# Cross-attention and feed-forward kernel: scores on four 32-row tiles, and PSUM dealt out anew

## The chip, the cores and the metric

The kernel runs on one core of one Trainium2 chip. A core has five engines that run side by side, each through its own queue in order: TensorE (PE, matrix products, which only it can write to PSUM), VectorE (DVE), ScalarE (ACT), GpSimd (POOL) and SyncE (SP, which here only issues DMAs). They are ordered among each other by semaphores alone. The metric is the device time of one execution, in microseconds.

## The reference, cut to what matters

16 batches (B) of 128 positions and 128 features; 8 heads of 16 features. The first part is an mLSTM cell with q = layernorm(x) and k = v = ctx, the second a feed-forward net with weights +1 and -1.

```python
log_f = jax.nn.log_sigmoid(fg)                  # gates from q, k, v
cs = jnp.cumsum(log_f, axis=1)
log_D = where(tril, cs[:, :, None] - cs[:, None, :], -inf) + ig[:, None, :]
max_log_D = jnp.max(log_D, axis=-1, keepdims=True)
D_mat = jnp.exp(log_D - max_log_D)
qk = jnp.einsum('hsd,htd->hst', qh, kh) / np.sqrt(DH)
C = qk * D_mat
normalizer = jnp.maximum(jnp.abs(C.sum(-1, keepdims=True)), jnp.exp(-max_log_D))
h = jnp.einsum('hst,htd->hsd', C / (normalizer + EPS), vh)
x = x + (h - mean(h)) / sqrt(var(h) + 1e-5) * ln_scale
x = x + ffn(layernorm(x))     # [x, -x] -> 512 -> relu -> 512 -> relu -> 128
```

## The kernel before

Everything is written out by hand: each engine has its own program, and each instruction that needs another engine's result waits on a semaphore by count. The 16 batches go through a software pipeline of 23 slots (`for n in range(SLOTS)`). In slot n, PE makes the scores of batch n and the weighted values of batch n-1 and turns them back (transposes them); ACT makes the exponentials of batch n+1; DVE multiplies scores and exponentials of batch n (make_c) and then normalizes batch n-1 and adds batch n-2 to the residual.

**Groups.** The gates are made for four batches at a time (group g). turn(g, 1) and turn(g, 0) transpose ctx and the normalized x of the four batches on PE into PSUM, turn_out on ACT copies them to qcT. gates(g) on PE makes the gate rows, forget_min(g) on DVE takes min(f, 0), gate_logs(g) on ACT the abs, exp and ln of log-sigmoid, gate_scans(g) on DVE the two running sums and maxima, turn_a and turn_m transpose the two results, take_a, take_m and em_guard on ACT copy them out. The DMA queue of SP spreads the eight heads of q into q_heads and the running maxima to all partitions (maxb). For the first four batches (DIRECT) the maxima are not loaded by DMA: bar and spread_max lay the distances into PSUM on PE, and ACT's decay reads them there. Group 2 is turned in slot 3, its gates stand in slot 4, its scans in slot 4, its turn_a and turn_m in slot 5; group 3 the same in slots 7, 8 and 9.

**Scores.** scores(n), L386 to L398: two products, each over a 64-row tile of q_heads (four heads laid out in blocks), 512 columns wide, fp32, into the two banks of pS. Each fp32 product is two passes in the profile (64 records for 32 products).

**PSUM.** Eight banks: pG (transposes and gates), pS (two), pO (weighted values and what is turned back), pX (x2's transposes and one bank of the direct distances), pF (three, for the feed-forward sums, which take them in turn, L242). The direct distances of two batches at a time lie in pF and pX.

**Feed-forward part.** Pair f (two batches) has five sums ffn(f, m): m = 0, 1 the first layer, 2, 3 the second, 4 (LAST) the third; ffn_of_slot says in which slot each stands: (f-1, 3), (f, 0), (f, 1) in the slot that opens a pair, then (f-1, LAST), (f, 2). ACT's high(f, m) writes the relu as fp16, DVE's low(f, m) the rest. Before it DVE's norm_x makes x2, ACT's x2_take_high and POOL's x2_take_low split it, turn_x2(n) on PE transposes one batch a slot, and take_x2T(f) on DVE (L824) copies a pair to SBUF.

The order on each engine in a slot is that of its loop: PE L506 to L535, ACT L648 to L676, DVE in the loop behind gate_scans(0), POOL at the end.

## Time and profile before

| | us |
|---|---|
| Three runs | 126.08, 124.39, 125.08 (median 125.08) |
| The profiled execution: its time | 124.36 |
| Its span, first to last instruction | 122.6 |
| PE busy | 106.3 |
| DVE busy | 98.6 |
| ACT busy | 77.1 |
| POOL busy | 62.9 |
| Mean granted clock of TensorE | 0.968 |

The span is 1.8 us shorter than the execution's own time, which has a start and an end around it. Busy times count records of the engine that do not overlap; they say nothing about which engine another waits for. "Idle before" in a row is the time the engine stood still before that instruction, with the one that released it. The granted clock is a share of 2.4 GHz; 0.5 is 1.2 GHz.

### The profile page before, as it was taken

The page shows a single profiled execution, that of the slowest core. Times are in us where ns is not written, and L with a number is a line of the kernel's source. Part 1 is how long each engine was busy: PE and PEld are TensorE (multiplying, and loading weights), DVE is VectorE, ACT ScalarE, POOL GpSimd, SP SyncE. Part 2 cuts the span into 40 slices and gives each one's busy share as a digit, 9 for nine tenths or more (in the row PEclk, how much of TensorE's full clock was granted, in tenths as well). Part 3 has the DMA queues.
Part 4 walks back from the last instruction along what each step waited for, and adds up shares of the span by engine and source line. Part 5 has one row for each costly group of instructions (what it writes and reads, how often), then busy time and mean ns, then how long its engine had stood idle before and what let it go on. Part 6 is the DMA issues. An engine that isn't in the chain of part 4 may idle for free.

```text
span 122.6 us, 3374 instructions
## 1 busy us (share of the span) xinstructions
PE 106.3 (87%) x1127; PEld 75.1 (61%) x1127; DVE 98.6 (80%) x334; ACT 77.1 (63%) x227; POOL 62.9 (51%) x145
## 2 busy tenths in 40 slices
PE   4898999998486379999979999999999999898960
PEld 4897676473242143658665685765866767696950
DVE  5445977969699999783999799999899999847341
ACT  4013589468899673959597996986987352525110
POOL 6944770345738788282736484684661464520000
PEclk9999999999999955899999999999999999999998
DMA  2885375269213179001215970100100100110101
GB/s 68 229 225 113 53 215 120 48 227 372 88 25 58 47 318 322 32 0 22 50 22 154 331 268 1 43 8 0 43 5 0 43 0 8 43 43 0 51 0 43
DMA packets 13105, 11.45 MB, mean 93 GB/s; under 512 B 2064, under 2 KB 11552, under 8 KB 13088
## 3 DMA queue, kind: packets, MB, share of 16 engines
q1 hardware_dynamic: 11792, 10.82, 29.4%
q10 hardware_dynamic: 1296, 0.42, 1.5%
q8 instruction: 9, 0.15, 0.4%
q14 instruction: 8, 0.07, 0.2%
HBM read 8.94 MB, written 1.25 MB: 83 GB/s over the span
## 4 chain that ended last, share of the span: by engine, by line
POOL 42%; issue 28%; PE 19%; DVE 7%; ACT 1%; POOLq 1%; DVEq 0%
POOL maxb L975 10%; POOL rs_x L946 7%; POOL rs_h L946 6%; PE pF L468 6%; POOL x2p L994 5%; PE pF L376 4%; POOL rs_q L956 3%; PE pS L396 3%; POOL ve_x L945 3%; POOL ve_h L945 2%; PE pF L447 2%; POOL vals L967 2%; POOL q_heads L1022 1%; DVE xn L714 1%; DVE h L842 1%
## 5 line engine op out<-in xcount | busy, mean ns | idle before, releaser
L468 PE MATMUL pF<-h,w 128*128 128x256 f16 x256 | 30.3, 273 | 0.0
L599 ACT ACTIVATE dmat<-maxb,aT 128x128 f32<-128x128 f32 x96 | 29.3, 390 | 0.0
L468 PEld LDWEIGHTS pF<-h,w 128*128 128x128 f16 x256 | 24.7, 98 | 2.6
L842 DVE SCALAR_TENSOR_TENSOR h<-pF,h 128x512 f16<-128x512 f32 x32 | 20.9, 680 | 5.8 <-ACT h L622 5.8
L622 ACT ACTIVATE h<-pF 128x512 f16<-128x512 f32 x32 | 18.1, 591 | 9.8 <-PE pF L468 9.8
L748 DVE SCALAR_TENSOR_TENSOR cmat<-pS,dmat 128x512 f32<-128x512 f32 x32 | 20.5, 682 | 1.9 <-PE pS L396 1.9
L994 POOL TENSOR_TENSOR x2p<-x,x2p 128x128 f16<-128x128 f32 x16 | 6.9, 428 | 26.5 <-ACT x2p L614 26.5
L396 PE MATMUL pS<-q_heads,qcT 64*128 64x512 f32 x64 | 19.0, 672 | 0.0
L410 PEld LDWEIGHTS pO<-cmat,vals 128*32 128x32 f32 x256 | 6.3, 112 | 11.8 <-issue 9.9
L975 POOL TENSOR_SCALAR_AFFINE_SELECT maxb<-maxb 128x1024 f32<-128x1024 f32 x12 | 13.2, 1099 | 0.4 <-DMA maxb<-running_max 0.4
L410 PE MATMUL pO<-cmat,vals 128*32 128x128 f32 x256 | 10.7, 287 | 1.7 <-POOL vals L967 1.7
L608 ACT COPY oT<-pO 128x256 f32<-128x256 f32 x16 | 6.0, 372 | 8.5 <-PE pO L410 8.4
L460 PE MATMUL pF<-x2T,w 128*128 128x256 f16 x64 | 9.1, 290 | 1.3 <-DVE x2T L828 1.3
L447 PE MATMUL pF<-w,h 128*128 128x128 f16 x128 | 8.6, 219 | 1.8 <-DVE h L842 1.8
L946 POOL TENSOR_TENSOR rs_x<-ve_x,minus_half 128x1 f32<-128x1 f32 x16 | 9.4, 586 | 1.3
L946 POOL TENSOR_TENSOR rs_h<-ve_h,minus_half 128x1 f32<-128x1 f32 x16 | 8.9, 558 | 1.3
L614 ACT CAST x2p<-x 128x128 f16<-128x128 f32 x16 | 4.7, 294 | 7.3 <-DVE x L821 7.3
L551 ACT COPY qcT<-pG 128x512 f32<-128x512 f32 x6 | 3.6, 592 | 8.7 <-PE pG L337 8.7
L447 PEld LDWEIGHTS pF<-w,h 128*128 128x128 f16 x128 | 7.4, 98 | 2.4 <-DVE h L842 2.4
L475 PE MATMUL pF<-ident 128*128 128x128 f32 x44 | 7.4, 332 | 1.7 <-POOL ident L1011 1.7
L417 PE MATMUL pO<-ident,oT 128*128 128x128 f32 x32 | 6.7, 292 | 2.4 <-ACT oT L608 2.3
L460 PEld LDWEIGHTS pF<-x2T,w 128*128 128x128 f16 x64 | 6.2, 102 | 3.4 <-issue 2.3
(109 smaller groups left out, 185.2 us busy)
## 6 DMA issues: line engine op xcount, KB each, us to landing
maxb<-running_max SPq DMA_DIRECT2D x12, 512.0 KB, 5.9
xs<-in_x SPq DMA_DIRECT2D x4, 256.0 KB, 5.0
out<-outb SPq DMA_DIRECT2D x8, 128.0 KB, 1.8
q_heads<-qcT SPq DMA_DIRECT2D x30, 32.0 KB, 2.0
cs_in<-in_ctx SPq DMA_DIRECT2D x3, 256.0 KB, 4.7
cs_in<-in_ctx ACTq DMA_DIRECT2D x1, 256.0 KB, 4.2
k_in<-in_L_ffn_k SPq DMA_DIRECT2D x1, 256.0 KB, 6.0
running_max<-max_row SPq DMA_DIRECT2D x3, 64.0 KB, 1.8
```

Source lines behind the costliest of these rows:

```text
L396: pe.matmul(pS[:, 4 * half:4 * half + 4].rearrange("p h s -> p (h s)"), qcT[rows, g % 2, j, 1], q_heads[rows, g % 2, j].rearrange("p h s - ...
L410: last = pe.matmul(pO[32 * i:32 * i + VW, half], vals[:, n // GB % 2, n % GB, h], cmat[:, n % 2, h], start=True, stop=True)
L447: last = pe.matmul(bank[:, 0, D * j:D * (j + 1)], h2[:, k, part, S * j:S * (j + 1)], w2[:, k], start=(k == 0 and part == 0), stop=(k == FT ...
L460: last = pe.matmul(bank[:, u], w0[:, columns], x2T[:, f % 2, part], start=(part == 0), stop=(part == 1))
L468: last = pe.matmul(bank[:, u], w1[:, k, columns], h1[:, k, part], start=(k == 0 and part == 0), stop=(k == FT - 1 and part == 1))
L599: last = act.activation(dmat[:, n % 2, h], source, ACT.Exp, bias=aT[:, g % 2, j, h:h + 1], scale=-1.0)
L622: act.activation(hidden(f, m, 0), ffn_place(f, m), ACT.Relu).then_inc(ffn_high, 1)
L748: dve.scalar_tensor_tensor(out=cmat[:, n % 2, part].rearrange("p h s -> p (h s)"), in0=pS[:, part].rearrange("p h s -> p (h s)"), scalar=Q ...
L842: dve.scalar_tensor_tensor(out=hidden(f, m, 1), in0=ffn_place(f, m), scalar=0.0, in1=hidden(f, m, 0), op0=ALU.max, op1=ALU.subtract).then_ ...
L946: return pool.tensor_tensor(dst, work, minus_half[:, :], ALU.pow)
L975: pool.affine_select(out=maxb[:, g % 2, j], in_=maxb[:, g % 2, j], compare_op=ALU.is_ge, fill=NEVER, base=0, pattern=[[0, NH], [1, S]], ch ...
L994: pool.tensor_tensor(x2p[:, n % 2, 1], x2[:, n % 2], x2p[:, n % 2, 0], ALU.subtract).then_inc(x2_low, 1)
```

## The change

- Scores: four products on tiles of 32 rows, two heads (256 columns) each, each into a bank of its own; pS grows from two banks to four, pG and pX go.
- The feed-forward sums get fixed banks of pF. Transposes, gates and the direct distances go into pF in the time before; the direct distances have one set of two banks for all batches, so bar and spread of a batch wait for ACT's reads of the one before, half by half.
- x2 is turned by pairs: four transposes in the slot that opens a pair; x2p has four places. take_x2T goes from DVE to ACT, between take_o and the exponentials.
- Group 3 is turned in slots 4 and 5, its gates are made in slot 6 (behind weigh(5)), its scans in slot 6, turn_a and turn_m in slot 7. qcT, aT and em have three places.
- min(f, 0) becomes relu(-f) on ACT within gate_logs; the signs in gate_scans follow. A small instruction on DVE makes the negative bias.

```diff
+QT = 4
+QH = NH // QT
...
-        pG = ps("pG", [128, 4, S])
-        pS = ps("pS", [128, NH, S])
+        pS = ps("pS", [128, QT, 4, S])
         pO = ps("pO", [128, 4, S])
-        pX = ps("pX", [128, 2 * TOK], F32)
         pF = [ps(f"pF{i}", [128, 2, TOK], F32) for i in range(FB)]
...
-            return pF[SUMS.index((f, m)) % FB][:, :]
+            return pF[0 if (f, m) == (NF - 1, LAST) else {0: 1, 1: 0, 2: 1, 3: 2, LAST: 2}[m]][:, :]
...
+        def direct_place(n, h):
+            return whole(pF[h // 4])[:, h % 4]
...
+            return whole(pF[{(0, 1): 1, (0, 0): 2}.get((g, part), 1 - part)])
+
+        def gate_place(g):
+            return whole(pF[2])[:, 0:2]
...
+        x2_turn = pF[0][:, 0].bitcast(F16).rearrange("p (e t) -> p e t", e=2)
...
+            def bar(n, half):
+                if n >= 1:
+                    pe.wait_ge(direct_read, 2 * (n - 1) + half + 1)
+                pe.matmul(whole(pF[half]), ident_b[:, :], above[:, :].unsqueeze(1).broadcast_to([128, 4, S]),
+                          start=True, stop=False)
...
-                for half in range(2):
-                    if n >= 1:
-                        pe.wait_ge(c_ready, 2 * (n - 1) + half + 1)
-                    rows = slice(64 * half, 64 * (half + 1))
-                    pe.matmul(pS[:, 4 * half:4 * half + 4].rearrange("p h s -> p (h s)"), qcT[rows, g % 2, j, 1],
-                              q_heads[rows, g % 2, j].rearrange("p h s -> p (h s)"),
-                              start=True, stop=True).then_inc(scores_ready, 1)
+                for q in range(QT):
+                    if n >= 1 and q % 2 == 0:
+                        pe.wait_ge(c_ready, 2 * (n - 1) + q // 2 + 1)
+                    rows = slice(32 * q, 32 * (q + 1))
+                    last = pe.matmul(pS[:, q, 0:QH].rearrange("p h s -> p (h s)"), qcT[rows, g % 3, j, 1],
+                                     q_heads[rows, g % 2, j].rearrange("p h s -> p (h s)"), start=True, stop=True)
+                    if q % 2 == 1:
+                        last.then_inc(scores_ready, 1)
...
+            def turn_x2(f):
+                pe.wait_ge(x2_low, FG * (f + 1))
+                if f == 0:
+                    pe.wait_ge(turned_out, 7)
+                else:
+                    pe.wait_ge(ffn_low, hidden_to(f - 1, 1))
+                for j in range(FG):
+                    for part in range(2):
+                        last = pe.transpose(x2_turn[:, part, S * j:S * (j + 1)], x2p[:, (FG * f + j) % (2 * FG), part],
+                                            ident16[:, :])
                 last.then_inc(x2_turned, 1)
...
-            bar(0)
-            bar(1)
+            bar(0, 0)
+            bar(0, 1)
...
-            spread_max((0, 1), 0)
-            spread_max((0, 1), 1)
+            spread_max(0, 0)
+            spread_max(0, 1)
             turn_m(0)
             gates(1)
             scores(0)
-            bar_and_spread(2)
+            bar_and_spread(1, 0)
+            bar_and_spread(1, 1)
...
+                if n in (1, 2):
+                    bar_and_spread(n + 1, 0)
+                if n == 3:
+                    turn(2, 0)
+                if n == 6:
+                    gates(3)
+                if n == 4:
+                    turn(3, 1)
+                if opens_pair(n):
+                    turn_x2((n - FFN_LAG) // FG)
+                if n == 5:
+                    turn(3, 0)
                 for f, m in early:
                     ffn(f, m)
                 if 0 <= n - 1 < B:
                     turn_o(n - 1)
-                if n == 1:
-                    bar_and_spread(3)
+                if n in (1, 2):
+                    bar_and_spread(n + 1, 1)
...
-                act.wait_ge(f_min_ready, g + 1)
-                step(act.activation(f_abs[:, :], pG[:, 1], ACT.Abs, bias=gate_b[:, 1:2]))
+                act.wait_ge(gates_ready, g + 1)
+                if g >= 1:
+                    act.wait_ge(a_ready, g)
+                step(act.activation(f_abs[:, :], gate_place(g)[:, 1], ACT.Abs, bias=gate_b[:, 1:2]))
+                act.activation(f_drop[:, :], gate_place(g)[:, 1], ACT.Relu, bias=gate_b[:, 2:3], scale=-1.0)
...
+            def take_x2T(f):
+                act.wait_ge(x2_turned, f + 1)
+                if f >= 2:
+                    act.wait_ge(ffn_sums, sums_to(f - 2, LAST // 2 - 1))
+                act.copy(x2T[:, f % 2], x2_turn).then_inc(x2T_ready, 1)
...
+                if n in (4, 6):
+                    gate_logs(n // 2)
+                if n in (5, 7):
+                    take_a((n - 1) // 2)
+                    take_m((n - 1) // 2)
+                    em_guard((n - 1) // 2)
+                if n == 3:
+                    turn_out(2, 1)
                 if 0 <= n - 1 < B:
                     take_o(n - 1)
-                if k == 3 and g + 2 < NG:
-                    turn_out(g + 2, 0)
+                if opens_pair(n):
+                    take_x2T((n - FFN_LAG) // FG)
...
+            step(dve.tensor_scalar(gate_b[:, 2:3], pF[0][:, 0, 6 * NH + 1:6 * NH + 2], -1.0, None, ALU.mult))
```

## Rows read from the trace of the kernel before

**Rows 1.** The page: busy time by engine; clock granted to TensorE, 40 slices.

```profile
PE 106.3 (87%) x1127; PEld 75.1 (61%) x1127; DVE 98.6 (80%) x334; ACT 77.1 (63%) x227; POOL 62.9 (51%) x145
...
PEclk9999999999999955899999999999999999999998
```

**Rows 2.** Windows: stretch, length; busy of PE, PEld, DVE, ACT, POOL; clock, DMA.

```profile
17.71:28.82 11.11, 10.49 (x91) 6.24 (x87) 8.90 (x28) 7.89 (x28) 4.11 (x12) 1.00 0.56 165
28.82:44.36 15.54, 9.53 (x114) 4.86 (x114) 14.05 (x53) 13.73 (x45) 10.72 (x25) 0.96 0.37 121
44.36:50.05 5.69, 5.52 (x32) 2.52 (x33) 5.09 (x14) 2.86 (x9) 4.61 (x9) 0.52 0.75 275
50.05:72.60 22.55, 21.67 (x253) 15.33 (x251) 19.06 (x66) 18.70 (x59) 11.75 (x27) 1.00 0.37 111
72.60:101.98 29.38, 28.66 (x318) 20.25 (x317) 28.86 (x101) 20.77 (x62) 16.48 (x36) 1.00 0.06 18
```

**Rows 3.** Windows of two single pairs of batches, same columns.

```profile
73.80:83.25 9.45, 9.23 (x103) 6.31 (x102) 9.38 (x34) 7.65 (x25) 6.30 (x14) 1.00 0.06 16
83.25:93.00 9.75, 9.75 (x109) 6.80 (x108) 9.40 (x33) 8.23 (x27) 5.01 (x11) 1.00 0.05 15
```

**Rows 4.** Chain of waits from 14 us: start, us, what.

```profile
16.77 1.01 PE pG L347 x32
17.78 1.06 PE pS L396 x4
```

**Rows 5.** Line L396 from 84.1 us: min/median/max ns, first and last start.

```profile
L396 PE MATMUL pS<-q_heads,qcT x2: 693/693/693, 84.2 to 84.2; 64*128 64x512 f32 x2
```

**Rows 6.** Windows of line L376 alone (PE, PEld): one batch, then two.

```profile
19.30:21.28 1.98, 1.98 (x16) 1.85 (x16) 1.00 0.36 61
14.46:16.44 1.98, 1.98 (x32) 1.85 (x32) 1.00 0.30 55
```

**Rows 7.** Groups by form: busy us, mean ns of one | idle before, releaser.

```profile
L551 ACT COPY qcT<-pG 128x512 f32<-128x512 f32 x6 | 3.6, 592 | 8.7 <-PE pG L337 8.7
...
L828 DVE COPY x2T<-pX 128x512 f16<-128x512 f16 x8 | 3.3, 415 | 0.0
...
L556 ACT ACTIVATE f_abs<-pG,gate_b 128x128 f32<-128x128 f32 x4 | 1.5, 364 | 3.4 <-DVE f_min L719 3.4
...
L719 DVE TENSOR_SCALAR f_min<-pG,gate_b 128x128 f32<-128x128 f32 x4 | 1.4, 348 | 1.3 <-PE pG L347 1.3
```

**Rows 8.** Timeline of VectorE: start, us, what [idle before it, releaser].

```profile
8.63 0.15 DVE L877 COPY gate_b<-pF 128x2 f32<-128x2 f32 x1
...
50.25 0.17 DVE L761 SCALAR_TENSOR_TENSOR den<-pO,em 128x8 f32<-128x8 f32 x1 [0.60 <-PE pO L417]
...
53.34 1.28 DVE L748 SCALAR_TENSOR_TENSOR cmat<-pS,dmat 128x512 f32<-128x512 f32 x2
...
57.01 0.17 DVE L761 SCALAR_TENSOR_TENSOR den<-pO,em 128x8 f32<-128x8 f32 x1 [2.06 <-PE pO L417]
...
62.19 0.42 DVE L725 TENSOR_TENSOR_SCAN cumf<-f_min,f_ln 128x128 f32<-128x128 f32 x1
...
63.49 0.29 DVE L739 TENSOR_TENSOR m_row<-cumf,max_row 128x128 f32<-128x128 f32 x1
...
68.88 0.17 DVE L761 SCALAR_TENSOR_TENSOR den<-pO,em 128x8 f32<-128x8 f32 x1 [0.65 <-PE pO L417]
```

**Rows 9.** Timeline of TensorE matmuls.

```profile
46.15 2.08 PE L396 MATMUL pS<-q_heads,qcT 64*128 64x512 f32 x4
48.16 1.08 PE L410 MATMUL pO<-cmat,vals 128*32 128x128 f32 x16
...
106.76 0.27 PE L427 MATMUL pX<-ident,x2p 128*128 128x128 f16 x2 [0.59 <-POOL x2p L994]
```

**Rows 10.** Waits of VectorE, 48.3 to 102 us: total, times, longest.

```profile
DVE den L761 <- PE pO L417: 3.6, 4, 2.1
DVE h L842 <- ACT h L622: 0.3, 1, 0.3
```

More of the change, by code:

```diff
@@ L77, with opens_pair @@
 HIDDEN_SUMS = [at for at in SUMS if at[1] < LAST]
+def opens_pair(n):
+    return (n - FFN_LAG) % FG == 0 and 0 <= n - FFN_LAG < B
 def sums_to(f, m):
@@ L107, in xattn_ffn @@
         bias_in = sb("bias_in", [NH, 2])
-        gate_b = sb("gate_b", [128, 2])
+        gate_b = sb("gate_b", [128, 3])
         lns = sb("lns", [128, D])
@@ L211, in xattn_ffn @@
         direct_spread = sem("direct_spread")
+        direct_read = sem("direct_read")
         c_ready = sem("c_ready")
@@ L346, in gates @@
                         for j in range(GB):
-                            last = pe.matmul(pG[32 * j:32 * j + VW, n], w[:, n, :], qcT[:, g % 2, j, part],
+                            last = pe.matmul(gate_place(g)[32 * j:32 * j + VW, n], w[:, n, :], qcT[:, g % 3, j, part],
                                              start=(part == 0), stop=(part == 1))
@@ L361, in turn_m, with spread_max, bar_and_spread @@
                 pe.transpose(am_place(g)[:, 1], m_row[:, :], ident[:, :]).then_inc(am_turned, 1)
-            def bar(n):
-                if n >= 2:
-                    pe.wait_ge(exp_ready, n - 1)
-                for half in range(2):
-                    pe.matmul(direct_place(n, half), ident_b[:, :], above[:, :].unsqueeze(1).broadcast_to([128, 4, S]),
-                              start=True, stop=False)
-            def spread_max(batches, half):
-                pe.wait_ge(max_ready, 1)
-                for i in range(4):
-                    h = 4 * half + i
-                    for n in batches:
-                        rows = slice(32 * n, 32 * (n + 1))
-                        last = pe.matmul(direct_place(n, half)[:, i],
-                                         ident[rows, 32 * n + h:32 * n + h + 1].broadcast_to([32, 128]),
-                                         max_row[rows, 0], start=False, stop=(i == 3))
+            def bar(n, half):
[3 more added lines that the diff above has]
+                          start=True, stop=False)
+            def spread_max(n, half):
+                pe.wait_ge(max_ready, 1)
+                rows = slice(32 * n, 32 * (n + 1))
+                for h in range(4 * half, 4 * half + 4):
+                    last = pe.matmul(direct_place(n, h), ident[rows, 32 * n + h:32 * n + h + 1].broadcast_to([32, 128]),
+                                     max_row[rows, 0], start=False, stop=(h % 4 == 3))
                 last.then_inc(direct_spread, 1)
-            def bar_and_spread(n):
-                bar(n)
-                for half in range(2):
-                    spread_max((n,), half)
+            def bar_and_spread(n, half):
+                bar(n, half)
+                spread_max(n, half)
             def scores(n):
@@ L523, in _ @@
                     turn_m(1)
-                if 0 <= n - 4 < B:
-                    turn_x2(n - 4)
-                if k == 3 and g + 2 < NG:
-                    turn(g + 2, 0)
+                if n in (1, 2):
[10 more added lines that the diff above has]
+                    turn(3, 0)
                 for f, m in early:
@@ L881, in _ @@
             q_group(1)
-            forget_min(0)
             norm_group(1)
@@ L886, in _ @@
             ffn_weights_0_2()
-            forget_min(1)
             for n in range(SLOTS):
-                g, k = divmod(n, GB)
-                prepare = n < B and g + 1 < NG
                 before = ffn_of_slot(n - 1)[1]
@@ L895, in _ @@
                     low(f, m)
-                if prepare and k == 0 and n > 0:
-                    forget_min(g + 1)
                 if n < B:
@@ L902, in _ @@
                     norm_group(2)
-                if prepare and k == 0 and n > 0:
-                    gate_scans(g + 1)
-                if (n - FFN_LAG) % FG == 0 and 0 <= n - FFN_LAG < B:
-                    take_x2T((n - FFN_LAG) // FG)
+                if n in (4, 6):
+                    gate_scans(n // 2)
                 q_at = q_statistics(n + 3 * GB)
```

170 lines of the change are left out of this document (76 added, 94 removed).

## Prediction

> **What bounds the kernel now.** I read the page first [rows 1]: TensorE (PE) busy for 87% of the span, VectorE (DVE) for 80%, and a TensorE clock that falls to about half in two of the 40 slices. That is an average, so next come the engines by stretch [rows 2], cut where batches hand over. Up to 28.82 us PE leads (10.49 of 11.11 us busy). From 28.82 to 44.36 DVE leads (14.05 of 15.54) and PE idles. From 44.36 to 50.05 the granted clock is 0.52, the level of 1.2 GHz: PE is busy nearly throughout because its work takes twice as long. From 50.05 to 72.60 PE is full (21.67 of 22.55) and DVE has 3.5 us free. From 72.60 to 101.98 both are full (28.66 and 28.86 of 29.38). After that the last batches drain. Two single pairs of batches in the full stretch [rows 3] say it most sharply: 9.45 and 9.75 us, in which DVE is busy 9.38 and 9.40, PE 9.23 and 9.75, ACT only 7.65 and 8.23. So the change has to take time from both PE and DVE; whichever keeps more is the next bound.
>
> **Scores on 32-row tiles.** Before, each batch's scores take 1.06 us on PE [rows 4]: two 64-row tiles, 512 columns each, two passes per product. The two tiles start together (both records at 84.2) [rows 5], so four passes of 512 columns cost the time of two, 0.53 us per pass. Four tiles of 256 columns are four pairs of half-length passes; if all four run side by side the cost is 2 x 0.27 = 0.53 us, a gain of 0.53 per batch. Nothing in the trace runs four row tiles at once. The nearest row runs two of 32 rows: 32 passes of spread_max for two batches took the 1.98 us that 16 passes for one batch take [rows 6]. Bounds: 0.53 if all overlap, 8 x 0.27 = 2.1 if none do. I take 0.53, because every pair of row tiles in the trace overlapped wholly. Against it the Trainium skill (TensorE: Matmul & The Clock Gate, "Measured speedup vs the span model") measured 3.07 times, not 4, for four row tiles; by that the scores would take 0.7 us, and as PE is not the bound after the change the sum would stay.
>
> PE per pair of batches then is 9.75 - 2 x 0.53 = 8.7, at most.
>
> **DVE's relief.** take_x2T leaves DVE: 415 ns each, 8 of them, of which I count 0.38, since the next instruction starts a little before one ends; forget_min leaves it too, 348 ns x4 [rows 7], counted 0.3. A pair of batches then costs DVE 9.45 - 0.38 = 9.07. That is above PE's 8.7, so DVE is the next bound and the scores' saving does not come through in full. make_c reads the same number of elements from two banks instead of one; I cost that at nothing (bounds 0 and +0.05 each).
>
> **What ACT gets.** Eight x2T copies at the size of the 592 ns qcT copy, four Relus at the 364 ns of f_abs [rows 7]. It has 1.5 to 1.8 us free per pair [rows 3], which covers 0.6. If that cover were gone each would be paid in full. The Trainium skill speaks against the move (ScalarE: Activation LUTs, "Rules for kernel authors": relu, min and the like belong on VectorE). The rows agree that the copy itself is dearer, 592 against 415 ns; by the rule alone eight copies would cost 1.4 us more. The sum goes by which engine is full, and that is DVE.
>
> **By stretch, against the profiled execution** (span 122.6, its time 124.36):
>
> Up to 17.71: one more small DVE instruction behind gate_b, in front of what gates(0) and group 1's statistics wait for; 0.15 long, 0.19 from start to start [rows 8]. The forget_min that goes was done in the wait for POOL. +0.2. Bounds 0 and +0.3.
>
> 17.71 to 44.36: the direct distances lose their second pair of banks. spread_max(0, 1), which did two batches in 1.98, becomes two calls of 1.98 [rows 6], so PE gets +2.0, and three extra orderings (bar and spread wait for ACT's reads). Four batches' scores give 2.1 back. ACT's decay(1) and decay(2) start about 0.5 and 0.4 later. It meets the DVE-led stretch from 28.82, in which PE idles 6 us [rows 2] and so also covers group 3's first transposes. Net 0; bounds -1.0 (turn(2, 0) no longer waits for turn_out(2, 1)) and +1.5 (ffn_weights_1, behind decay on ACT, pushes everything after it).
>
> 44.36 to 53.34, the start of make_c(7) [rows 8]: here group 3 is made, in front of a PE at half clock. In slot 6 the order is scores(6), weigh(5), gates(3). Scores at half clock take 2.08, now half of it; weigh 1.08 [rows 9]. From 46.15: 47.2, 48.2, then gates(3), 1.01 at full clock [rows 4] and 2.0 at half: 50.2. ACT must do gate_logs(3) (four ACTIVATEs at about 0.35: 51.5) before take_o(5); DVE does gate_scans(3), 1.5 us (62.19 to 63.7 now, in slot 8 [rows 8]), up to 53.0, before it turns to normalizer(5). That started at 50.25 before [rows 8]: 2.75 later, of which the 0.3 that DVE waited for high(0, 2) in this slot [rows 10] is absorbed. So make_c(7) moves from 53.34 to about 55.7: +2.4. What is queued behind the new wait: turn_o(5) and the first ffn of the second layer behind it on PE, decay(7) on ACT. Bounds +0.8 (clock does not fall) and +4.
>
> 53.34 to 72.60, make_c(7) to the start of make_c(10): DVE loses its waits 2.06 and 0.65 [rows 8], forget_min 0.3, gate_scans(3) 1.5, two x2T copies 0.76: 5.2. PE's side allows it: it drops three scores (1.6), group 3's eight transposes and gates (2.2). I leave 0.5 for new waits: -4.7. Bounds -5.2 and -1.5 (the waits come back, behind other work).
>
> 72.60 to 101.98 (norm_x(13)): three copies, 1.14, and the last DVE wait, 0.28; the waits for turn_o sum to 3.6 from 48.3 on [rows 10]: -1.4. Bounds -1.8 and -0.6.
>
> 101.98 to the end: products of the feed-forward part follow on PE almost without a gap, and no scores are left. The 0.59 in which it waited for one batch's x2 [rows 9] goes, since pairs are turned a slot later: -0.6. Bounds -1.2 and 0.
>
> Sum: 0.2 + 0 + 2.4 - 4.7 - 1.4 - 0.6 = -4.1. Against 124.36 that is 120.3, against the median 125.08 it is 121.0. The profiled run is at the low end of the three (124.39 to 126.08), so I say 120.6.
>
> **Rivals.** (a) *The DVE waits only move.* Only DVE instructions count: six copies and one forget_min, -2.5, tail -0.6, start +0.2, and 0.9 lost in slot 6 (2.4 less the scans' 1.5): -2.0, about 123.0. For it: ACT now does gate logs, x2T and turn_out before each take_o and decay in slots 4 to 7. Against: two engines with 1 us per pair free each. (b) *The clock holds.* Without the half-clock stretch at 44 us slot 6 costs 0.8, not 2.4, and ffn(0, 0), ffn(0, 1) end 0.9 sooner: about 118.5. For it: group 3's transposes fill PE's idle time in front of it. Against: the scores, halved, empty it by as much. (c) *Slower: more stretches at 1.2 GHz.* PE has more gaps, waiting for DVE. The one stretch seen was preceded by 15.54 us with PE 61% busy [rows 2]; it cost half of its 5.5 busy us, 2.7. One more, in slots 7 to 16, costs 2.7 less PE's new slack of 0.3; it takes two to cancel the gain, and three put it at about 128. Against: PE stays about 95% busy there. (d) *The four row tiles take turns.* Then a batch's scores cost 2.1, PE costs 8.7 + 2 x 1.6 = 11.9 per pair, 2.8 above DVE's 9.07, and over five pairs that gives about 134. Against: rows 5 and 6. (e) ACT becomes the bound in slots 3 to 7, +2 on my sum: 122.8, counted with (a).
>
> **How the numbers follow.** Forecast 0.55; (a) with (e) 0.20; (b) 0.15; (c) 0.06; (d) 0.04. A measurement tells about 2% from no change: 122.6 is the line for faster. The forecast and (b) lie below it but for the forecast's upper end, (a) about half: faster 0.79, same 0.13, slower 0.08. The range holds (b) and (a): 117.8 to 124.0; the forecast's own is 119 to 122.5.
>
> **What would show it.** L396's successor: 0.5 to 0.6 us per batch on PE, 1.06 would put PE at the bound again, 2 is (d). DVE over 95% busy from slot 7 to 16, in pairs of about 9.1 us, with PE waiting for c or x2T. A DVE wait of 1 to 2 us for f_ln in slot 6, behind gates(3) on PE and gate_logs on ACT. A granted clock near 0.5 for one stretch near 44 us only. I am wrong if pairs in slots 10 to 16 last 9.4 or more, if a second half-clock stretch shows, or if make_c(4) starts over 1 us later than before.

## The result, and the profile after

The changed kernel has a median of 121.62 us (four runs: 120.66, 121.34, 121.9, 123.23) beside 125.09 for the kernel before (four runs, 124.39 to 126.08): a ratio of 0.969, 95% interval 0.959 to 0.979. The profiled execution took 120.66 us with a span of 118.8 (before: 124.36 and 122.6). Repeated beside other experiments it had a median of 121.85. Medians are of all runs, ratios and their intervals of the fast runs alone (within 1.5% of the kernel's fastest), and where too few of those were left no ratio is given. Single runs of each kernel lie 2 to 3 us apart. Two things that vary from run to run come up in the last sections (how long TensorE runs at half clock, and how fast its first products go), so the experiments are read by stretches of their traces as well as by medians.

Three of the 52 runs of the changed kernel and the kernels made from it took far longer: 131.23 (the changed kernel repeated), 131.52 and 130.07, with a mean granted clock of 0.88 to 0.89. None of the 61 runs of the kernel before and the kernels made from it did. None of the three was traced, so where their time went is open.

The page of the changed kernel, its busy times and the row of the granted clock, answer to [rows 1]:

```profile
PE 100.9 (85%) x1191; PEld 77.0 (65%) x1191; DVE 95.8 (81%) x323; ACT 81.5 (69%) x239; POOL 62.6 (53%) x145
...
PEclk9999999999999976999999999999999999999998
```

PE lost 5.4 us, DVE 2.8, ACT gained 4.4. The dip in the clock is still there, but two slices of 0.7 and 0.6 instead of 0.5 and 0.5. The windows by stretch, cut at the same events as [rows 2] where they exist: scores(0), make_c(4), make_c(7), make_c(10), norm_x(13), the end (stretch, length; busy of PE, PEld, DVE, ACT, POOL; clock, DMA share, GB/s):

```profile
17.78:36.65 18.87, 17.25 (x213) 11.85 (x210) 16.11 (x56) 16.22 (x53) 9.08 (x23) 1.00 0.54 163
36.65:53.67 17.02, 12.15 (x154) 7.75 (x152) 16.16 (x52) 14.72 (x49) 11.59 (x25) 0.90 0.47 139
53.67:69.03 15.36, 14.42 (x186) 11.19 (x184) 14.16 (x48) 14.53 (x46) 10.65 (x25) 1.00 0.56 168
69.03:98.03 29.00, 26.74 (x337) 20.49 (x336) 28.18 (x99) 21.70 (x64) 16.62 (x36) 1.00 0.06 16
98.03:118.80 20.77, 15.44 (x162) 12.98 (x159) 10.80 (x27) 7.37 (x15) 3.62 (x9) 0.98 0.09 26
```

PE is no longer full in the long stretch (26.74 of 29.00); DVE is (28.18). make_c(7) starts at 53.67 (53.34 before), make_c(10) at 69.03 (72.60), norm_x(13) at 98.03 (101.98). So a gain of 3.9 us, as much as the whole, falls between make_c(7) and make_c(10), and the three pairs of batches behind it, where both engines had been full, give 0.4 together.

Two single pairs of batches, same columns, answering to [rows 3]:

```profile
69.03:78.47 9.44, 8.86 (x114) 6.72 (x113) 9.19 (x33) 8.32 (x27) 6.52 (x15) 1.00 0.05 16
78.47:87.97 9.50, 8.87 (x114) 6.70 (x113) 9.21 (x33) 8.19 (x26) 5.95 (x12) 1.00 0.06 16
```

The scores' line, L403, from 80.1 us (duration min/median/max, first and last start), and the groups by form of the scores and the x2T copy, answering to [rows 5] and [rows 7]:

```profile
L403 PE MATMUL pS<-q_heads,qcT x4: 478/478/478, 80.1 to 80.1; 32*128 32x256 f32 x4
```

```profile
L403 PE MATMUL pS<-q_heads,qcT 32*128 32x256 f32 x128 | 12.8, 437 | 0.0
L638 ACT COPY x2T<-pF 128x512 f16<-128x512 f16 x8 | 4.7, 586 | 0.0
```

All four tiles start together. From one batch's first product to the next work on PE it is 0.65 us (85.01 to 85.65), where it was 1.06.

VectorE's waits from 48 to 98 us (total, times, longest), answering to [rows 10]:

```profile
DVE den L793 <- PE pO L425: 1.6, 5, 0.9
DVE cumf L754 <- ACT f_ln L580: 0.2, 1, 0.2
```

The four waits for turn_o, 0.60, 2.06, 0.65 and 0.28, became one of 0.92 and four of 0.18.

### The profile page after: what moved, and what is told of

It is laid out like the page before. It is cut to its first block, busy times and chain, and to the rows that moved or that the text cites. A ratio compares the mean times of both kernels' runs of the same rounds, so it can differ in the third digit from the quotient of the medians.

```text
span 118.8 us, 3484 instructions
## 1 busy us (share of the span) xinstructions
PE 100.9 (85%) x1191; PEld 77.0 (65%) x1191; DVE 95.8 (81%) x323; ACT 81.5 (69%) x239; POOL 62.6 (53%) x145
## 4 chain that ended last, share of the span: by engine, by line
POOL 39%; issue 24%; PE 18%; DVE 9%; DMA 3%; ACT 3%; POOLq 1%; DVEq 0%
POOL maxb L994 10%; POOL rs_x L965 7%; POOL rs_h L965 6%; PE pF L480 6%; POOL x2p L1013 5%; PE pF L385 5%; DMA xs<-in_x 3%; POOL rs_q L975 3%; POOL ve_x L964 3%; PE pF L459 3%; POOL ve_h L964 2%; POOL vals L986 2%; DVE h L868 2%; DVE xn L748 2%; PE pS L403 1%
## 5 line engine op out<-in xcount | busy, mean ns | idle before, releaser
L403 PE MATMUL pS<-q_heads,qcT 32*128 32x256 f32 x128 | 12.8, 437 | 0.0
L621 ACT ACTIVATE dmat<-pF,aT 128x128 f32<-128x128 f32 x32 | 9.0, 371 | 3.4 <-PE pF L385 2.1
L385 PE MATMUL pF<-max_row,ident 32*128 32x128 f32 x64 | 9.0, 281 | 0.1
L385 PEld LDWEIGHTS pF<-max_row,ident 32*128 32x128 f32 x64 | 7.6, 184 | 2.0 <-issue 1.6
L487 PE MATMUL pS<-ident 128*128 128x128 f32 x44 | 7.4, 332 | 1.7 <-POOL ident L1030 1.7
```

The costliest lines, as they stand in the source:

```text
L385: last = pe.matmul(direct_place(n, h), ident[rows, 32 * n + h:32 * n + h + 1].broadcast_to([32, 128]), max_row[rows, 0], start=False, stop ...
L403: last = pe.matmul(pS[:, q, 0:QH].rearrange("p h s -> p (h s)"), qcT[rows, g % 3, j, 1], q_heads[rows, g % 2, j].rearrange("p h s -> p (h ...
L621: last = act.activation(dmat[:, n % 2, h], source, ACT.Exp, bias=aT[:, g % 3, j, h:h + 1], scale=-1.0)
```

## The experiments

Stretches below are named by the make_c that bounds them: c4 to c7 is the start of make_c(4) to the start of make_c(7). Each median is of six runs. The kernel before, run among the three sets (11 runs in each), had medians of 125.09, 125.24 and 125.21.

**The changed kernel once more**, as the measure of the others.

> The changed kernel once more, as the anchor of this set of runs on one chip. Theory and rivals alike: a ratio to the kernel before of 0.965 to 0.975; pairs of batches of 9.4 to 9.5 us in slots 10 to 15.

Median 121.85, ratio 0.967 [0.959, 0.974]. c4 to c7 17.24 us (17.02 in the first profile), c7 to c10 15.05 (15.36), from make_c(0) to the end 99.87 (100.19). But make_c(0) itself starts at 19.93 instead of 18.61: the start varies by more than most effects sought here. Its pairs:

```profile
70.25:79.54 9.29, 8.85 (x114) 6.71 (x113) 9.04 (x33) 8.31 (x26) 6.75 (x15) 1.00 0.05 16
79.54:89.03 9.49, 8.86 (x114) 6.70 (x113) 9.21 (x32) 8.31 (x26) 6.17 (x13) 1.00 0.06 16
```

The first is 0.15 shorter than in the first profile; none of its residuals meets GpSimd's mask (see the section on the hardware).

**turn_o between the halves of the last ffn product of the pair.** In slots that open a pair, turn_o(n−1) moves forward by half an ffn.

```diff
-            def ffn(f, m):
+            def ffn(f, m, between=None):
...
+                        if u == 0 and between is not None:
+                            between()
...
-                for f, m in early:
-                    ffn(f, m)
-                if 0 <= n - 1 < B:
+                split = 0 <= n - 1 < B and bool(early) and early[0][1] == 3
+                for f, m in early:
+                    ffn(f, m, (lambda: turn_o(n - 1)) if split else None)
+                if 0 <= n - 1 < B and not split:
                     turn_o(n - 1)
```

> The changed kernel with turn_o(n-1) put between the two halves of ffn(f-1, 3) in the slots that open a pair. Theory P (a loop through pO sets the pair: head_out(n-2) frees pO, then weigh(n-1), turn_x2, the whole of ffn(f-1, 3), turn_o(n-1), normalizer(n-1), head_out(n-1)): the wait of DVE for turn_o, 0.18 a pair, goes, residual starts earlier and no longer meets POOL's mask; pairs fall from 9.45 to 9.1 us, the whole by 1.5 to 2.5 us. Rival Q (VectorE's own instructions set the pair): at most the 0.18 per pair, under 1 us in the whole. Rival R (POOL's mask is met at another place): pairs stay at 9.4.

Median 121.42, ratio 0.966 [0.960, 0.972], no clear difference from the changed kernel's 0.967; make_c(0) to the end 99.08, 0.79 under the repeated changed kernel, whose trace has a stretch at half clock where this one has none. Its pairs:

```profile
70.28:79.47 9.19, 8.84 (x114) 6.70 (x113) 9.12 (x32) 8.30 (x26) 6.58 (x15) 1.00 0.06 16
79.47:88.89 9.42, 8.88 (x114) 6.72 (x113) 9.32 (x33) 8.34 (x27) 6.11 (x13) 1.00 0.06 17
```

The waits of 0.18 are gone (from 50 to 98 us DVE waits for no other engine at all), and the two pairs are 0.25 and 0.08 shorter than in the changed kernel's first profile, 0.10 and 0.07 shorter than in its repetition. The wait for turn_o was real, but of rival Q's size; the 1.5 to 2.5 us of theory P did not come. In each of these pairs one residual (L837, 0.35 alone) now takes 0.54, beside GpSimd's mask; in the changed kernel only the first of its two pairs had that (0.50), and in its repetition neither. So DVE's own work is 9.19 - 0.19 = 9.00 in one pair and 9.42 - 0.19 = 9.23 in the other.

**The x2T copy back on VectorE**, from the changed kernel.

```diff
-                act.copy(x2T[:, f % 2], x2_turn).then_inc(x2T_ready, 1)
+                dve.tensor_copy(x2T[:, f % 2], x2_turn).then_inc(x2T_ready, 1)
```

> The changed kernel with the eight x2T copies back on VectorE behind make_c. Theory P: VectorE waits 0.18 for turn_o just behind that place in each pair, so a copy of 0.38 costs 0.2 a pair, and the whole grows by 1 to 1.5 us. Rival Q (VectorE's work alone sets the pair): 0.38 a pair and 8 copies, +3 us. Rival S (the move is worth nothing because TensorE sets the pair): within 0.5 us of the changed kernel.

Median 122.99, ratio 0.970 [0.962, 0.978]: 1.1 above the changed kernel beside it, 0.94 from make_c(0) to the end. Of that 0.84 lies in c4 to c7 (18.08 against 17.24), where this run also had a longer stretch at half clock (41.6 to 48.5 us; 44.1 to 47.5 in the other). Its pairs last 9.44 and 9.36 (9.29 and 9.49 without the copy), so in the full stretch the copy costs nothing that shows: DVE's waits for turn_o, 0.18 a pair, are gone, and theory P's 0.2 a pair is not there either. By the ratios (0.970 against 0.967, the intervals overlap) the whole difference is 0.5 us. So the copies are worth 0.5 to 1.1 us, none of it clear of the spread, and how much of it is the copy and how much the longer stretch isn't separated.

**Two 64-row tiles again**, from the changed kernel, in its new PSUM layout.

```diff
-                for q in range(QT):
...
+                for half in range(2):
+                    rows = slice(64 * half, 64 * (half + 1))
+                    pe.matmul(pS[:, half].rearrange("p h s -> p (h s)"), qcT[rows, g % 3, j, 1],
+                              q_heads[rows, g % 2, j].rearrange("p h s -> p (h s)"),
+                              start=True, stop=True).then_inc(scores_ready, 1)
```

> The changed kernel with the scores as two products on 64-row tiles again, everything else as changed. If the four tiles carry the gain: scores back at 1.06 from 0.64 us, TensorE at 8.9 + 0.85 = 9.7 us per pair, full, and about 0.25 to 0.3 per pair longer from slot 7 on; with slots 5 to 9 the whole grows by 2 to 3.5 us and most of the gain over the kernel before is gone. Rival: the gain comes from group 3's earlier place and the moved copies, then this costs under 1 us.

Median 123.08, ratio 0.981 [0.976, 0.986]: 1.2 above the changed kernel by medians, 1.8 by the ratios (whose intervals do not meet), 0.7 from make_c(0) to the end, most of it (0.5) in c0 to c4, where PE is full. The last is a lower bound: this trace has no stretch at half clock near 44 us, the repeated changed kernel's has one. Two of the three measures lie between the theory's 2 to 3.5 us and the rival's under 1. The pairs:

```profile
71.07:80.52 9.45, 9.45 (x106) 6.66 (x105) 9.08 (x33) 8.32 (x27) 6.54 (x15) 1.00 0.06 16
80.52:90.02 9.50, 9.50 (x106) 6.66 (x105) 9.21 (x32) 8.35 (x27) 6.13 (x13) 1.00 0.06 16
```

PE is full to the last hundredth, and the pairs last as long as with four tiles in the first profile (9.44 and 9.50) and 0.16 and 0.01 longer than in the repetition. This is the sharpest line on the new tiles: in the full stretch they free 0.6 us of PE per pair and shorten next to nothing, since DVE with its small losses comes to nearly the same.

**Only the copies and the minimum on ScalarE**, in the kernel before.

```diff
-                dve.tensor_copy(x2T[:, f % 2], x2_turn[:, f % 2]).then_inc(x2T_ready, 1)
+                act.copy(x2T[:, f % 2], x2_turn[:, f % 2]).then_inc(x2T_ready, 1)
...
+                act.activation(f_min[:, :], pG[:, 1], ACT.Relu, bias=gate_b[:, 2:3], scale=-1.0)
```

> The kernel before with the x2T copies and min(f, 0) on ScalarE and nothing else. TensorE is full before in slots 10 to 15 (9.5 us per pair), so if TensorE and VectorE are level there, relief of VectorE alone gives next to nothing: pairs of 9.4 to 9.5 us, the whole within 1 us of before. Rival (VectorE's own work was the bound before): 0.38 per pair and the copies in slots 5 to 9, 2 to 3 us faster.

Median 122.90 against 125.24, ratio 0.987 [0.966, 1.007]. The medians are 2.3 apart, but the runs of both spread too far for the interval to leave out zero. The trace has c4 to c7 in 15.63 (16.60 before) and c7 to c10 in 18.27 (19.26), only 0.3 less behind make_c(10), and 1.0 more in c0 to c4 (18.78 against 17.79), where its clock was at 0.50 up to 36.5 us, which the trace before doesn't have. From make_c(0) to the end it is 102.35 against 103.65, 1.3 less. "Within 1 us of before" was too little, the rival's 2 to 3 us isn't shown; the pairs (9.54 and 9.41) are as expected.

**Only group 3 made early**, in the kernel before: turned in slot 5, gates and scans in slot 6, turn_a and turn_m in slot 7, three places for qcT, aT and em. The place isn't quite the changed kernel's: there half of the transposes stand in slot 4 and the gates behind weigh(5), here all transposes stand in slot 5 and the gates ahead of scores(6).

```diff
-                if prepare and k == 0 and n > 0:
-                    gates(g + 1)
+                if n in (4, 6):
+                    gates(n // 2)
...
-                if k == 3 and g + 2 < NG:
-                    turn(g + 2, 1)
+                if n in (3, 5):
+                    turn((n + 1) // 2, 1)
```

> The kernel before with one part of the change: group 3 turned in slot 5, its gates and scans in slot 6, turn_a and turn_m in slot 7, with three places for qcT, aT and em; scores, PSUM, x2 and the split between ACT and VectorE as before. Theory G (the place of group 3 carries the gain: slots 7 to 9 were where both engines waited in turn, slots 4 and 5 had room on TensorE): make_c(4) to make_c(10) falls from 35.9 to about 33 us, the whole by 2.5 to 3.5 us, ratio about 0.975. Rival H (it needs the faster scores too, since TensorE is full from slot 6 on before): slots 4 to 10 fall by under 1.5 us, ratio 0.99 or more.

Median 126.71 (one run of 123.43, five from 126.5 to 127.7), against 125.24 for the kernel before. The profile is of the one short run, no ratio is given, and the five long runs have no trace, so a loss of 1.5 isn't shown. The trace has 18.63 in c4 to c7 (16.60 before) and 15.61 in c7 to c10 (19.26), and from make_c(0) to the end 102.73 against 103.65. So the early place alone takes 3.65 us out of c7 to c10, nearly all that the change takes there (its shorter stretch at half clock, 43.8 to 47.2 us, may have a part in it), and gives 2.0 back in c4 to c7, where PE waits 2.2 us with turn(3) for ACT to empty pG. What the rest of the change decides is how much of the 3.65 is kept.

**Products that keep TensorE busy**, in the changed kernel: seven 128x128 products in front of weigh(4), two behind turn(3, 1), their result unused.

```diff
+                if n == 5:
+                    fill(7)
                 if 0 <= n - 1 < B:
                     weigh(n - 1)
...
                     turn(3, 1)
+                    fill(2)
```

> The changed kernel with filler products on TensorE where it waits in slots 4 and 5 (2 and 7 products of 128 columns into a bank that is free), to see what the stretch at 1.2 GHz near 44 us costs. Theory (VectorE leads there and TensorE has room): the granted clock stays at 1.0 and the whole falls by under 0.7 us. Rival (the half-clock stretch is on the path): make_c(4) to make_c(7) falls from 17.1 by over 1 us, the whole by as much.

Median 121.08 (one run of 131.52 among the six), ratio 0.981 [0.967, 0.994]. The mean granted clock is 1.00, with no dip in any slice, and c4 to c7 is 17.10, as in the changed kernel with its dip (17.02, 17.24). There the half clock costs nearly nothing; from make_c(0) to the end it is 99.68 against 100.19 and 99.87. The pairs are 9.30 and 9.51.

**turn_o moved as above, and the mask in two halves**, the second behind x2_take_low on GpSimd.

```diff
-                mask(n + 2)
+                mask(n + 2, 0)
...
                     x2_take_low(n - 3)
+                mask(n + 2, 1)
```

> The changed kernel with turn_o(n-1) between the halves of ffn(f-1, 3) and POOL's mask split into two halves of four heads, the second behind x2_take_low. With turn_o moved alone a pair took 9.19 and 9.42 us, and residual on VectorE was stretched from 0.35 to 0.44 in the mean where it meets the mask. If that meeting is the rest of the gap to 9.05, pairs of 9.05 to 9.2 us and 1.5 to 2.5 us less than the changed kernel over the whole. Rival (the stretch has another cause, or only moves to other instructions): pairs of 9.3 to 9.45, the whole as with turn_o alone, within 0.5 us.

A miss. Median 122.74, ratio 0.981 [0.950, 1.011], the c4 to c7 stretch 18.88 instead of 17.10. The longest waits of VectorE and TensorE from 37 to 58 us:

```profile
DVE x L837 <- POOL rs_h L968: 1.2, 2, 1.0
...
PE pO L425 <- ACT oT L635: 2.8, 2, 1.7
PE pO L418 <- POOL vals L989: 2.3, 1, 2.3
```

On GpSimd's timeline the copy of vals (42.22) stands right behind half a mask (41.63, 0.65 long), and PE's weigh waits 2.3 us for it, where the longest such wait of the changed kernel was 1.7; turn_o then waits for ACT. The pairs behind got no shorter either (c10 to c14 19.11, against 18.61 with turn_o alone). This kernel had a second dip of its clock near 17 us as well, and the trace is of one of its four runs near 122.8; the other two, 120.84 and 121.01, are no longer than those of turn_o alone. So no gain shows anywhere, against the 1.5 to 2.5 us expected; whether the split costs the 1.8 isn't settled.

**The kernel before and the changed one, each with its clock held.** Four kernels with the same fillers in slots 4 and 5, and four instead of eight filler products behind turn(0, 1): the kernel before, the changed one, the changed one with turn_o in between, and the kernel before with copies, minimum and group 3's early place, so all of the change but the tiles, the new PSUM layout and x2 by pairs.

```diff
             turn(0, 1)
-            keep_busy(8)
+            keep_busy(4)
```

> The kernel before with two things that should take the clock out of the comparison: 4 filler products instead of 8 ahead of turn(0, 0), and 2 and 7 filler products on TensorE where it waits in slots 4 and 5. Theory K (the stretch at 1.2 GHz near 44 us costs the kernel before about 2 us, and a slow start of the filler products 1.6 us): granted clock 1.0 or near it in nearly all runs, median 122.4 (span 120.6), 2.5 us under before. Rival (the stretch is hidden): within 0.7 us of before.

> The changed kernel with the same two things. Theory K (of the 3.4 us that the change gained, about 1.4 are that the half-clock stretch became shorter and met more slack; 2 are its structure): median 119.9 to 120.2 (span 118.1 to 118.4), 2.0 to 2.5 us under f1. Rival (all of the gain is structure): 3.3 us or more under f1. Rival (all of it was the clock): within 1 us of f1.

> f2 with turn_o between the halves of ffn(f-1, 3). By the profile of that edit alone (99.1 against 100.0 us from make_c(0) to the end): 0.7 to 1.1 us under f2, median 119.0 to 119.3. Rival: the gain was the clock's and the two are equal within 0.4 us.

> f1 with two parts of the change: the x2T copies and min(f, 0) on ScalarE, and group 3 made in slots 5 to 7; scores on two 64-row tiles, PSUM and x2's turning as before. Copies alone came out 1.5 to 1.9 us faster at like clock, group 3 alone not faster. If these two carry the structural gain between them: median 120.4 to 121, within 0.7 us of f2. If the scores and the new PSUM layout carry most of it: 1.2 us or more above f2.

The first has a median of 122.76 (122.1 to 123.7), 2.45 under the kernel before, by nine small products added and four taken out. From make_c(0) to the end the traces say the same: 101.35 against 103.65, 2.3 less. The kernel before without fillers had 4 of its 33 runs in these sets at a clock of 1.00: 122.09 and 122.43, as short as with fillers, but also 124.48 and 124.68, which were not traced. The second has 120.05, 1.8 under the changed kernel's 121.85; the third 119.66 (five runs from 119.0 to 120.6 and one of 130.1), 0.4 under the second by medians, less than the 0.7 to 1.1 expected, and 0.7 from make_c(0) to the end (98.50 against 99.23), with pairs of 9.19 and 9.41 against 9.44 and 9.50; the fourth 125.18. No ratios are given for these four, so they are read against each other. The windows of the first, c4 to c7, c7 to c10, c10 to norm_x(13):

```profile
36.67:52.00 15.33, 13.24 (x134) 8.07 (x122) 14.93 (x49) 12.65 (x42) 11.90 (x26) 1.00 0.52 156
52.00:70.30 18.30, 17.43 (x211) 12.64 (x210) 16.34 (x56) 15.41 (x49) 10.75 (x25) 1.00 0.46 133
70.30:99.66 29.36, 28.65 (x318) 20.31 (x317) 28.83 (x101) 20.77 (x62) 16.48 (x36) 1.00 0.07 21
```

and of the second:

```profile
36.58:53.66 17.08, 13.50 (x177) 9.85 (x176) 16.34 (x52) 15.38 (x52) 11.98 (x26) 1.00 0.51 142
53.66:68.50 14.84, 13.90 (x180) 10.73 (x178) 14.15 (x48) 14.05 (x44) 10.81 (x24) 1.00 0.53 172
68.50:97.49 28.99, 26.73 (x337) 20.47 (x336) 28.18 (x98) 21.82 (x64) 16.85 (x37) 1.00 0.06 16
```

With the clock at 1.00 in both, the change costs 1.75 in c4 to c7, gives 3.46 in c7 to c10 and 0.37 behind it; by medians it is worth 2.7, above theory K's 2.0 to 2.5 and below the rival's 3.3. The fourth takes 21.33 in c4 to c7 and 14.99 in c7 to c10. Its median is 5.1 above the second's, as foreseen for the case that tiles and layout carry the gain, but also 2.4 above the first's, a loss that wasn't foreseen. Its waits of VectorE and TensorE from 36 to 58 us:

```profile
DVE den L770 <- PE pO L417: 3.6, 1, 3.6
...
PE pG L337 <- ACT em L587: 2.2, 1, 2.2
PE pO L417 <- ACT oT L617: 2.0, 2, 1.4
```

turn(3) needs the bank pG, which turn_a and turn_m of group 2 fill and ACT empties; PE waits 2.2 us for it in slot 5, the granted clock is down to 0.50 behind the wait, the seven fillers behind the wait take 2.78 us, and DVE waits 3.6 for turn_o behind all of that. In the changed kernel the transposes of group 3 go to other banks than the gates, and its trace from 36 to 54 us has no wait of turn(3) for ACT; the rest of the 6 us against the first of the four isn't taken apart. Part of the 21.33 is the fillers' own: without them the single move had 18.63. Group 3 also stands at slightly other places in slots 4 to 6 than in the changed kernel, as said above, so layout and order aren't separated. Two kernels that would separate more were not run: the fourth without fillers, and the changed kernel with group 3 at its old place.

## Why the prediction was right, and where it was not

The time (120.6 said, 121.6 measured, 120.66 in the profiled execution) lies in the forecast's range, but it is a sum of terms of which some missed against each other. Event by event, profiled executions:

| stretch | predicted | before to after | clock held in both |
|---|---|---|---|
| up to scores(0) | +0.2 | +0.07 | +0.43 |
| on to the first ffn product (44.36 before) | 0 | -0.70 | -0.94 |
| on to make_c(7) | +2.4 | +0.96 | +2.17 |
| make_c(7) to make_c(10) | -4.7 | -3.90 | -3.46 |
| on to norm_x(13) | -1.4 | -0.38 | -0.37 |
| to the end | -0.6 | +0.15 | +0.07 |
| span | -4.1 | -3.8 | -2.1 |

That the sum came out right is in part luck: the term of slot 6 was 1.4 too high and that of the stretch to the first ffn product 0.7, and the last three terms together promised 2.6 more than came.

**Scores.** "If all four run side by side the cost is 0.53": they do, rival (d) falls, and the size is 0.65. Four passes of 512 columns' worth one after another would be 2.1, so four tiles gave 3.3 times. By the figure of the Trainium skill (TensorE: Matmul & The Clock Gate, "Measured speedup vs the span model": 3.07 times for four row tiles, 512 columns each) 0.7 was the estimate; the trace, with 256 columns, lies nearer to it than to mine. As the prediction said, nothing hung on it in the full stretch. The experiment with two tiles puts the whole worth of the tiles at 0.7 us by stretches, 1.2 by medians and 1.8 by ratios.

**Slot 6: the step that failed.** The prediction put gates(3) at half clock, ending at 50.2, and normalizer(5) 2.75 later. The granted clock by windows of 1 us (same columns as the windows above), first the changed kernel:

```profile
45.00:46.00 1.00, 1.00 (x7) 0.59 (x9) 1.00 (x6) 1.00 (x5) 0.41 (x2) 0.50 1.01 303
46.00:47.00 1.00, 1.00 (x24) 0.51 (x24) 0.96 (x5) 1.00 (x4) 0.62 (x2) 0.83 1.18 262
47.00:48.00 1.00, 1.00 (x40) 0.81 (x32) 1.00 (x3) 0.17 (x1) 0.76 (x3) 1.00 0.83 258
```

and the kernel before:

```profile
46.00:47.00 1.00, 1.00 (x4) 0.51 (x4) 0.96 (x7) 1.00 (x3) 0.69 (x2) 0.50 0.80 311
47.00:48.00 1.00, 1.00 (x4) 0.00 (x0) 1.00 (x3) 0.12 (x1) 0.79 (x3) 0.50 1.01 356
48.00:49.00 1.00, 1.00 (x18) 0.59 (x16) 0.84 (x3) 0.00 (x0) 0.96 (x2) 0.50 0.99 299
```

The fall came at 43 us in both. The return to 2.4 GHz came at about 46.3 instead of 49.9. What brought it back is open. From 43.73 on PE has no gap until the gates are done, where before it had idled 0.84 in front of the same ffn product (at 44.36, waiting for x2T on DVE); but the kernel before with only the copies moved has no such gap either, and its clock stays at 0.50 up to 50 us. The short stretch isn't the change's alone: the changed kernel with the copies back had the long one (41.6 to 48.5), the kernel before with only group 3 early a short one (43.8 to 47.2). The timeline of the changed kernel shows what came of it:

```profile
45.55 1.08 PE L403 MATMUL pS<-q_heads,qcT 32*128 32x256 f32 x8
...
47.68 0.40 PE L359 MATMUL pF<-qcT,wkv 128*32 128x128 f32 x8
...
49.49 0.43 DVE L754 TENSOR_TENSOR_SCAN cumf<-f_drop,f_ln 128x128 f32<-128x128 f32 x1 [0.24 <-ACT f_ln L580]
...
51.00 0.16 DVE L793 SCALAR_TENSOR_TENSOR den<-pO,em 128x8 f32<-128x8 f32 x1
```

Scores are at half clock, weigh already at full, and the last of the gates starts at 47.68. The scans start at 49.49 with a wait of 0.24, not the 1 to 2 us foreseen, and normalizer(5) at 51.00, 0.75 later than before. The order of the chain (gates, logs, scans, normalizer) was the one named, but its gates, foreseen to end at 50.2, ended at 48.1: scores(6) started 0.6 earlier than the 46.15 taken over from the kernel before, and the other 1.5 is the half clock, which had been copied over at its old length.

Beside that, the kernel before paid for its own dip, which the prediction used in rival (b) only for the changed kernel. With the clock held, the kernel before gains 1.27 in c4 to c7 (16.60 to 15.33) and 0.96 in c7 to c10 (19.26 to 18.30, its wait of 2.06 for turn_o down to 1.09), 2.45 by medians. The changed kernel gains almost nothing of this in c4 to c7 (17.08 against 17.02 and 17.24). So of the measured 3.5 us some 2.1 (profiles) to 2.7 (medians) is the new structure, and the rest is that the half clock costs the changed kernel less: it is shorter in its traces, and PE has more slack there (busy 12.15 of 17.02 us in c4 to c7, 12.65 of 16.60 before). How much of this the change itself brought is not shown. Of rival (b) half came true: the clock didn't hold, it came back sooner. Its time did not: with the clock held the changed kernel has 121.08 and 120.05, not 118.5.

**make_c(7) to make_c(10).** -4.7 said, -3.9 found. The waits of 2.06 and 0.65 went, but 0.92 and 0.18 came in their place, 1.1 where 0.5 had been left for them; the other 0.2 isn't taken apart. The biggest term, and right in kind: DVE's waits, scans and copies leave a stretch where PE had been full, and PE's own share (three scores and group 3's products) left too. The single parts show whose it is: with group 3 early in the old layout the stretch falls by as much (15.61 alone, and 14.99 with copies and fillers, where the kernel with fillers alone has 18.30). The tiles hardly bear on it (15.13 with two, 15.05 with four). That the early place must be paid for in c4 to c7, and that the old layout pays more, is shown by 18.63 and 21.33 against 17.1 there; with fillers it makes a loss of the whole (125.18 against 122.76). That the new layout is what makes it cheaper is argued from the wait of 2.2 us for pG, and not shown apart from the order within the slots.

**The full stretch.** "I am wrong if pairs in slots 10 to 16 last 9.4 or more": they last 9.44 and 9.50 (9.29 and 9.49 in the repetition), so this step was wrong though DVE is the bound, as said (28.18 us of 29.00). Said was 9.07. PE does wait for DVE, as said, but for the low halves of the hidden layers (1.4 us from 69 to 98 us), not for c or x2T. The experiment with turn_o in between puts DVE's own work at 9.00 in one pair and 9.23 in the other, on both sides of 9.07; what wasn't counted is the wait for turn_o, 0.18 in each pair, and the residual held up by the mask, 0.15 in the first (9.44 - 0.18 - 0.15 = 9.11; in the repetition, which met no mask, 9.29 - 0.18 = 9.11 as well). Why the second pair is longer in both kernels isn't known. The wait is a loop that only appears when DVE is faster than the work in front of turn_o:

```profile
72.42 1.92 PE L480 MATMUL pF<-h,w 128*128 128x256 f16 x16
...
74.17 0.38 PE L425 MATMUL pO<-ident,oT 128*128 128x128 f32 x2
...
74.59 0.17 DVE L793 SCALAR_TENSOR_TENSOR den<-pO,em 128x8 f32<-128x8 f32 x1 [0.18 <-PE pO L425]
```

weigh, the transposes of the pair's x2 and a whole sum of the feed-forward part, ffn(f-1, 3), stand in front of turn_o; a PE that is 94% busy makes DVE wait. That is rival (a), that waits only move, on a small scale: 0.18 in each of four pairs. Of rival (c), more time at half clock, no trace shows anything in slots 7 to 16, but the three runs of 130 to 131.5 us at a clock of 0.88 to 0.89 fit it in time and clock, and no trace can say more.

**The tail.** -0.6 said, +0.15 found. The 0.59 for x2 did go, and another wait stands there:

```profile
102.91 1.07 PE L459 MATMUL pF<-w,h 128*128 128x128 f16 x16 [0.54 <-DVE h L868]
...
109.11 1.07 PE L459 MATMUL pF<-w,h 128*128 128x128 f16 x16 [0.54 <-DVE h L868]
```

The last product of a pair's feed-forward part needs DVE's low half of the product before; in the kernel before the first of these two waits was hidden behind the turned x2 (the products start at 106.89) and the second stood at 0.41 (at 112.96). "A stall goes, what is late next?" was asked of slot 6 and not of the tail.

**What ACT took over** (0.59 per copy, 0.37 per Relu) is covered, as said: no DVE wait for a copy appears, and one of 0.24 for f_ln. One instruction is dearer on ACT, the copy 0.59 against 0.41, the Relu 0.37 against the minimum's 0.35. The Trainium skill (ScalarE: Activation LUTs, "Rules for kernel authors") has relu and min on VectorE; it doesn't name copies. Its side of the price agrees with these rows. What the move of the copies was worth is the 0.5 to 1.1 us of the experiment that put them back, not clear of the spread; the Relu was never moved back by itself.

## What to carry to other kernels

Where two engines are full, taking time from one only shows how close the other is: price a relief by the next bound with its waits, not by the instruction that leaves (0.4 us came of 1.1 us of copies). A dip of the granted clock in a profile is itself a cost to be taken out before two kernels are compared; here nine small products in its way and four fewer at the start were worth 2.45 us to the kernel before (2.3 by traces), nearly as much as the restructuring (2.7 with them in both kernels), and 1.8 to the changed one (0.6 to 1.0 by traces from make_c(0)). The version with the change, those products and turn_o between the halves, at 119.66 us, beats both kernels. Work moved to an idle place needs a PSUM bank that is free there, or it waits for the engine that empties it, as turn(3) did for 2.2 us. And a forecast that is a sum of stretches is to be checked stretch by stretch: this one hit the total with a 1.4 us error in one term and 1.0 in another.

## What the runs showed of the hardware

**VectorE held up by GpSimd's mask.** The residual x<-hsc,rs_h,xs, both of whose 128-wide inputs lie in SBUF, takes 0.34 to 0.35 us; where the mask runs it takes up to 1.09. In the changed kernel, first GpSimd's timeline, then VectorE's:

```profile
33.89 1.10 POOL L994 TENSOR_SCALAR_AFFINE_SELECT maxb<-maxb 128x1024 f32<-128x1024 f32 x1
...
73.90 1.10 POOL L994 TENSOR_SCALAR_AFFINE_SELECT maxb<-maxb 128x1024 f32<-128x1024 f32 x1
```

```profile
34.04 1.09 DVE L834 SCALAR_TENSOR_TENSOR x<-hsc,rs_h,xs 128x128 f32<-128x128 f32 x1
...
74.89 0.50 DVE L834 SCALAR_TENSOR_TENSOR x<-hsc,rs_h,xs 128x128 f32<-128x128 f32 x1
```

The first starts 0.15 behind the mask and ends at 35.13, just after the mask's end at 34.99; the second meets only its last tenth and loses 0.15. make_c's products, which have one input in PSUM, keep their length wherever the mask runs (0.67 to 0.68 us for all 27 records from 27 us on). The Trainium skill (SBUF — State Buffer, "Who interferes with whom") says that a VectorE instruction with two SBUF inputs contends with a GpSimd instruction that reads SBUF, for a port pair that is an exclusive lock; the rows agree. It happens four times between 28 and 45 us in the changed kernel; twice the held instruction is xn<-xs, which has one such input (1.06 and 1.17 instead of 0.34), and the same section counts that form among those that can take the shared ports. In the full stretch before, the seven residuals took 0.35 to 0.39 from 72.6 us on. In the changed kernel it hangs on the run: one of seven takes 0.50 in the first profile and with the clock held, none in the repetition and with fillers alone, and that is the 0.15 by which their first pairs differ (9.44 and 9.44, 9.29 and 9.30). With turn_o in between one in each of the two pairs shown takes 0.54.

**The first products.** The same 16 filler products take 1.95 us in one run of the changed kernel (start 6.77), and this in its repetition:

```profile
7.39 3.18 PE L487 MATMUL pS<-ident 128*128 128x128 f32 x16
```

and 3.62 in the kernel with turn_o in between (start 7.35). Everything behind is later by that much (make_c(0) at 18.61, 19.93, 20.32), though the granted clock reads 1.00 in these slices. The start is slow in the traces of the changed kernel's repetition, of turn_o in between, of the copies put back and of two tiles, which were all run in one set, and in part with the clock held (scores(0) at 18.14 against 17.78); it is quick in the other four of the changed family and in all five of the kernel before and those made from it. Whether the change makes a slow start likelier isn't known, since no kernel of the older family was traced in that set, and what decides it stays open. Only differences from make_c(0) on are free of it.
